# Second attention layer of a two-layer gated block: three reorderings on VectorE, ScalarE and TensorE

## What is computed

```
x = x + tanh(g_xattn[0]) * L0_xattn(layernorm(x), ctx, bias, ...)
x = x + tanh(g_ffn[0])   * L0_ffn(layernorm(x), router, w1, w2)      # 64 experts, 4 per token
x = x + tanh(g_xattn[1]) * L1_xattn(layernorm(x), ctx, ln, Wq, Wkv, Wo, bo)
x = x + tanh(g_ffn[1])   * L1_ffn(layernorm(x), Wg, W_in, W_out)     # 8 experts, 2 per token
```

```
lat = layernorm(latents) * ln_l_w + ln_l_b;  ctx = layernorm(context) * ln_c_w + ln_c_b
q = lat @ Wq;  k, v = split(ctx @ Wkv)
attn = softmax(clip(q k^T / 8, -11, 11))
out = (attn v) @ Wo + bo
```

## Time and profile before

| | us |
|---|---|
| median of 3 runs | 2053.73 |
| range of the runs | 2053.43 to 2056.32 |
| profiled execution, its time | 2054.26 |
| profiled execution, its span | 2052.60 |
| TensorE busy in the span | 1805.4 (88%) |
| VectorE busy | 1244.4 (61%) |
| ScalarE busy | 902.4 (44%) |
| GpSimd busy | 600.8 (29%) |
| mean granted clock of TensorE | 0.946 of full |

### The profile page before, as it was taken

One profiled execution on the slowest core, in us unless ns is written; L12 is line 12 of the kernel. 1 busy time (PEld: TensorE's weight loads), 2 busy tenths in 40 slices (PEclk: granted clock), 3 DMA queues, 4 the chain that ended last, 5 costly groups with the idle time before them and its releaser, 6 DMA issues. The chain is left out here.

```text
span 2052.6 us, 47393 instructions
## 1 busy us (share of the span) xinstructions
PE 1805.4 (88%) x16643; PEld 1646.8 (80%) x16643; DVE 1244.4 (61%) x4006; ACT 902.4 (44%) x2276; POOL 600.8 (29%) x731
## 2 busy tenths in 40 slices
PE   5999999999997499967999988989998289999991
PEld 5899999899996388856888877878887189999991
DVE  2577777777777233335777766768776344554545
ACT  3777777777774133324443333423342033333330
POOL 0013223223223200024334343333421254445420
PEclk9999999999998699978999999999999689999996
DMA  6688011011000499972232111111100142222106
GB/s 204 235 273 290 27 37 42 26 36 40 26 25 27 153 296 295 295 239 79 88 105 69 48 44 49 38 43 52 51 28 23 57 158 92 88 79 83 52 32 251
DMA packets 134144, 214.13 MB, mean 104 GB/s; under 512 B 16878, under 2 KB 85009, under 8 KB 133952
## 3 DMA queue, kind: packets, MB, share of 16 engines
q1 hardware_dynamic: 106560, 147.89, 21.8%
q0 software_dynamic: 23040, 59.58, 9.1%
q10 hardware_dynamic: 4352, 4.20, 0.6%
HBM read 111.88 MB, written 103.68 MB: 105 GB/s over the span
## 5 line engine op out<-in xcount | busy, mean ns | idle before, releaser
L512 POOL DMA_INDIRECT buf<-a_rxn,a_disp x192 | 198.1, 1032 | 242.4 <-DVE comb L905 87.0
L646 ACT ACTIVATE a_S<-a_S,a_mn 128x128 f32<-128x128 f32 x512 | 198.9, 395 | 45.6 <-DVE a_mn L935 45.6
L82 PE MATMUL e_psH<-e_x_hi,e_w_hi 128*128 128x256 f32 x640 | 182.5, 285 | 0.0
L83 PE MATMUL e_psH<-e_x_lo,e_w_hi 128*128 128x256 f32 x640 | 179.3, 280 | 0.0
L84 PE MATMUL e_psH<-e_x_hi,e_w_lo 128*128 128x256 f32 x640 | 179.1, 280 | 0.0
L628 ACT ACTIVATE a_kT<-a_psP 128x512 f32<-128x512 f32 x128 | 75.7, 593 | 216.0 <-PE a_psP L84 216.0
L82 PE MATMUL a_psP<-a_c_hi,a_wk_hi 128*128 128x256 f32 x512 | 156.8, 306 | 9.1 <-DVE a_c_lo L797 9.0
L82 PE MATMUL a_psP<-a_x_hi,a_wq_hi 128*128 128x256 f32 x512 | 156.1, 305 | 5.2 <-DVE a_x_lo L797 5.2
L1225 PE MATMUL a_psM<-a_wo,a_oT 128*128 128x256 f32 x512 | 127.3, 405 | 30.8 <-ACT a_plain L589 23.4
L83 PE MATMUL a_psP<-a_c_lo,a_wk_hi 128*128 128x256 f32 x512 | 147.6, 288 | 0.0
L84 PE MATMUL a_psP<-a_c_hi,a_wk_lo 128*128 128x256 f32 x512 | 147.4, 288 | 0.0
(11 more groups left out here) (203 smaller groups left out, 5463.0 us busy)
## 6 DMA issues: line engine op xcount, KB each, us to landing
buf<-a_zeros SPq DMA_DIRECT2D x16, 1320.0 KB, 8.6
buf<-a_zeros SPq DMA_DIRECT2D x16, 1024.0 KB, 6.2
e_rows<-buf SPq DMA_DIRECT2D x64, 256.0 KB, 3.9
e_w_in<-in_L_ffn_w SPq DMA_DIRECT2D x64, 256.0 KB, 3.3
y<-e_y SPq DMA_DIRECT2D x64, 256.0 KB, 3.2
a_ctx<-in_ctx SPq DMA_DIRECT2D x32, 256.0 KB
e_w_out<-in_L_ffn_w SPq DMA_DIRECT2D x64, 128.0 KB, 3.8
y<-a_zeros SPq DMA_DIRECT2D x32, 256.0 KB, 2.4
```

Source lines behind the costliest of these rows:

```text
L82: pe.matmul(dst, a_hi, b_hi, start=start, stop=False)
L83: pe.matmul(dst, a_hi, b_lo, start=False, stop=False)
L512: g_.indirect_dma_start(out=buf, out_offset=bass.IndirectOffsetOnAxis(ap=disp[:, par, i, k:k + 1], axis=0), in_=rxn[:, par, i], in_offset= ...
L646: ins = a.activation(s[:, h], s[:, h], ACT.Exp, bias=mn[:, u % 2, h:h + 1], scale=-1.0, accum_out=z[:, u % 2, h:h + 1])
```

## The change

Three orders change in the second layer; the first layer keeps its own by `first`. No instruction is added or removed, and no wait.

- ScalarE, step 3: `evac_ctx` of group g + 2 comes before the first exponential, not behind it.
- VectorE: the residual update leaves the ends of steps 1 and 3 and comes behind the first reading of the scores in steps 2 and 0 (of the next group). In step 2 the router's moments come behind it, where they stood first in the step, and the router's normalisation comes behind the second reading, where it stood before it.
- TensorE: the weighing of both units comes ahead of the late projection, where it stood last in the step.

```diff
@@ ScalarE, step
                     evac_job(plus(g, 1), 1 - par, EARLY[w][0])
+                if not first and prep and w == 3:
+                    evac_ctx(plus(g, 2))
                 exponentials(g, 2 * w)
-                if prep and w == 3:
+                if first and prep and w == 3:
                     evac_ctx(plus(g, 2))
@@ VectorE, step
+            def update_earlier(g, w):
+
+                if w == 2:
+                    update_x(g, 1)
+                if w == 0:
+                    update_x(plus(g, -1), 3)
+
             def step(g, w, par, proj, prep):
                 if w == 0 and proj:
                     norm(plus(g, 1), NR - 1)
-                if w == 2 and routed(g, 1):
+                if first and w == 2 and routed(g, 1):
                     route_moments(plus(g, -1))
...
                 read_scores(g, 2 * w)
+                if not first:
+                    update_earlier(g, w)
+                    if w == 2 and routed(g, 1):
+                        route_moments(plus(g, -1))
                 if w == 0 and routed(g, 2):
                     route_shift(plus(g, -2))
                 if w == 2 and routed(g, 2):
                     route_read(plus(g, -2))
-                if w == 2 and routed(g, 1):
+                if first and w == 2 and routed(g, 1):
                     route_norm(plus(g, -1), 1 - par)
                 read_scores(g, 2 * w + 1)
+                if not first and w == 2 and routed(g, 1):
+                    route_norm(plus(g, -1), 1 - par)
...
-                    update_x(g, w)
+                    if first:
+                        update_x(g, w)
...
-                    update_x(g, w)
+                    if first:
+                        update_x(g, w)
@@ TensorE, step
                     turn_probs(g, 2 * w + 1)
+                else:
+                    weigh_turned(g, 2 * w, par)
+                    weigh_turned(g, 2 * w + 1, par)
                 if proj:
                     project(plus(g, 1), 1 - par, LATE[w])
...
                 project_out(g, w, proj, prep)
-                weigh = weigh_values if first else weigh_turned
-                weigh(g, 2 * w, par)
-                weigh(g, 2 * w + 1, par)
+                if first:
+                    weigh_values(g, 2 * w, par)
+                    weigh_values(g, 2 * w + 1, par)
```

## The result

The changed kernel takes 2074.08 us (median of 4 runs, 2073.89 to 2074.24), the kernel before 2055.03 on the same chip (2053.43 to 2059.28): 1.0094 times as long, with an interval of 1.0071 to 1.0118. It is slower by some 19 us, and above the range given. The profiled span went from 2052.6 to 2072.4 us.

A forecast was written before the change was run, and what follows sets the result against it. TensorE was taken to set the pace, with only its waits to win. Regular groups +16.8, first logits wait and drain +2.9, returns -18.0 and clock -2.8 summed to -1.1: 2053 us, no change, range 2043 to 2066.

The forecast's parts named there:

- Context ahead of the exponential: Step 3: the out-projection's 2.0 us wait for the context's evacuation loses its cause, by itself worth 23.4 us.
- third rival: Step 3: the heads also gate the out-projection, so its 2.0 wait stays and only the return is won; 2036, chance 0.06.
- Values ahead of the last projection: Step 3: the weighing now waits 2.1 us for the heads, replacing the 2.0 wait; +0.1 a group, wait bounds 1.5 and 2.6.
- second rival: Step 2: VectorE keeps its place, so the weighing's wait is 1.5, not 2.1, and the clock falls less; 2045, chance 0.2.
- Order on TensorE's own queue: A weighing between two projections adds a change of matmul kind; +0.1 a group, between 0 and 0.4.
- Update behind the next scores: Step 0: the router's logits wait for the update that reads their accumulator; +1.2 a group, bounds 0.8 and 1.6.
- the clock: Half clock behind the weighing's wait falls about as often, but the logits' wait hides most of it; -2.8 us.
- The ends: The first logits wait (group 2) and the drain, where routing lacks cover; +2.9 us, bounds 0 and 6.
- The loop's return: Three hardware-loop returns: the out-projection covers TensorE's compare-and-branch, while VectorE's later update costs 1.5 each; -18.0 us.
- first rival: At the loop's returns TensorE's branch is not covered, leaving a gap of over 3 us; +10.6, 2064, chance 0.22.

The follow-up runs named there:

- e8: The changed kernel with the logits of step 0 moved behind the weighing on TensorE; 2048.06 us, ratio 0.995 to the kernel before.
- e6: The changed kernel, but the update of step 3 stays at the end of its step; 2045.15 us, ratio 0.9938 to the kernel before.
- e9: The changed kernel with the second early projection of step 0 computed twice from group 2 on; 2068.93 us, ratio 1.0063 to the kernel before.
- e1: The kernel before with only the context's evacuation moved ahead of the exponential on ScalarE; 2023.18 us, ratio 0.9845.
- e4: The kernel before with context's evacuation and weighing moved, the update left at the end of its step; 2046.23 us, ratio 0.9954.
- e10: The kernel before with the last projection of step 3 computed twice in groups 2 to 13; 2045.95 us, ratio 0.9948.

## Why the prediction was wrong

The forecast was 2053, no change; the changed kernel is slower by 0.9%. The list of waits came out as foretold; the sum did not. By the spans the change was to give -1.1 and gives +19.8: the forecast was 20.9 too low. Groups 2 to 13 of the runs divide that up. They take 501.1 us before, 511.9 after, and 484.5 with the logits behind the weighing (e8).

- **Context ahead of the exponential**: right. Its wait lost its cause, and alone it gains 32.5; the third rival, in which the heads gate the out-projection, falls.
- **Values ahead of the last projection**: the wait stands where it was put, but is shorter, 1.3 to 1.9 instead of 2.1. TensorE gets there some 0.2 later than worked out, and the heads are as late as forecast (14.1) in four of the twelve groups only. In seven of the twelve the wait is under the 1.5 that the forecast named as a sign of being wrong. So much of the second rival came true; what it would have gained was lost in the next two terms.
- **Order on TensorE's own queue**: mis-sized. I took 0.1 a group between bounds of 0 and 0.4; group 1, without a wait, shows 0.83, some 0.2 in each of its four steps. It is the order alone: with only the context moved group 1 takes what it took before. Group 2 less its waits grew by as much (40.77 - 0.83 - 1.49 = 38.45, before 39.34 - 1.84 = 37.50). Over 12 groups that is 12 x 0.73 = 8.8 too little, partly made good by the shorter waits. Without the update's wait the groups gain 16.6 (501.1 - 484.5; e6, where that update stays in its place, has 484.8), where the forecast without it was -4.0 - 12 x 1.2 - 3 x 1.5 = -22.9. **6.3 too little**, a net that also holds what is left at the returns; the runs do not split it further.
- **Update behind the next scores, and the clock**: this step failed. In the sum the wait itself was nearly right, 20.2 us in groups 2 to 13 where 18.9 was forecast: 1.4 to 1.5 in groups 3, 4, 12 and 13 and 1.8 in groups 5, 7 and 9, where 1.2 was forecast with a bound of 1.6, and 2.4 to 3.0 behind the returns, where 1.2 + 1.5 = 2.7 was (groups 2 and 11 wait 0.8 and 0.2). The 0.4 more in groups 5, 7 and 9 comes from VectorE, whose product of the heads starts 0.5 behind its input there (1241.39 in the rows above) and at once in the groups written out; why was not settled. Together with the later VectorE at the returns it costs 504.5 - 484.5 = 19.9 in e9 against e8, where 12 x 1.2 + 3 x 1.5 = 18.9 was forecast. What was missed stands in the paragraph on the clock: I priced the half clock only behind the weighing's wait, and said that the logits' wait would swallow most of it. Where it did fall there, once, in step 3 of group 10, that came true: the step took 1.6 longer, and the logits of group 11 waited 0.2 instead of 1.8. But the logits' wait is itself a standstill of TensorE, with nothing behind it to take up a delay, and in five of the loop's groups (6 to 10) the clock fell right behind it. Price: 511.9 - 504.5 = 7.4. With 1.0 for the wait, **8.4 too little**. Step 0 was to take 9.6; away from the returns it mostly takes 10.2 to 10.6 at full clock, and 12.2 to 12.3 with the half clock.
- **The ends**, all that lies outside groups 2 to 13: 2.9 was forecast, for the drain and the first logits' wait; they cost 9.1, **6.2 too little**. Group 14 grew by 2.6, for it has the new order and a logits' wait of 1.5 like the others, and the sum of twelve groups left it out. Groups 0 and 1 grew by 3.1: 0.8 is the order in group 1, and some 1.7 is one step of group 0, where the clock fell in this execution (0.81 from 963 to 972). It fell there in e1, e4, e8, e9 and e10 too, and e10 is the kernel before up to group 2, so that is hardly the change's. From group 15 to the end of the span 3.5 are left, and whether they are the change's is not shown: that stretch takes 490.6 us in the kernel before and 493.5 in e10, 494.1 in the changed kernel and 497.4 in e9, with the same code there in each pair.
- **The loop's return**: the first rival falls, for the out-projection covers TensorE's branch. The three branches took 3.97, 3.50 and 3.64 us, 4.70 to 4.92 before. The Trainium skill (Advanced Engine Details and Errata, Control Flow Timing) gives a compare-and-branch about 108 ns. TensorE's rows do not agree, and to go by the row was right. The pairs of steps around a return still cost 3.2 more than a regular one of the groups written out, where 1.5 was forecast; in e9, without the half clock, 1.8. Steps 3 and 0 around the three take 78.2 us, against 87.17.

The three sums, 6.3 + 8.4 + 6.2, are the 20.9; no one of them alone would have left the range. The time lies 10 above the first rival's 2064, and came about in another way: not by a return left uncovered, but by a wait that was known and nearly rightly sized, and that was given no half clock.

## What to carry to other kernels

A wait that replaces another is not worth its length alone: ask what follows it on the same engine, and price the half clock at every standstill of TensorE, the new ones above all. A consumer that must wait can be put behind independent work on its own queue, with the chain that it waits for left as it is (here the logits behind the weighing, -26 us against the changed kernel). And try the parts of a change alone: here one part was worth 32 us, and the other two hid it.

## What had not been expected of the hardware

Doing more was faster: twelve matmuls added in each of twelve groups, in a wait, took 0.5% off the kernel before, since the out-projection behind that wait then kept the 2.4 GHz. Whether the clock falls does not follow from the length of a wait alone: behind 1.84 us in front of the logits of group 7 it fell, behind 1.81 in front of those of group 5 and behind 1.87 in front of the weighing in the group shown it did not, and behind 1.8 to 2.0 in the kernel before in five of twelve cases; what else decides was not settled. And a stop costs more than its idle time: without any half clock the logits' wait of 1.39 us in group 4 left step 0 1.63 longer than e8's, which has it filled (10.20 against 8.57).
